# Layer 0's tail: ScalarE normalises the next batch's x, each front has the bank of its own projection tile, and VectorE takes two modulations

## The reference, cut to what matters

```python
def _sln(h, w, ln_g, ln_b, Wg, bg, Wb, bb):          # layer norm, scaled and shifted by a condition
    mu = jnp.mean(h, axis=-1, keepdims=True)
    var = jnp.mean((h - mu) ** 2, axis=-1, keepdims=True)
    ln = (h - mu) / jnp.sqrt(var + EPS) * ln_g + ln_b
    gamma = (w @ Wg.T + bg)[:, None, :]
    beta = (w @ Wb.T + bb)[:, None, :]
    return gamma * ln + beta
h = _sln(hidden, w, ...)
qkv = (h @ Wqkv.T + bqkv)
...                                                  # attention, 16 heads of 32
out = out @ Wp.T + bp
h1 = out + hidden
h2 = _sln(h1, w, ...)
return h2 + h1
```

## Time and profile before

| | |
|---|---|
| median of three executions | 2795.2 us |
| profiled execution, its time | 2797.68 us |
| its span, first to last instruction | 2795.9 us |
| TensorE busy | 2621.9 us (94%) |
| VectorE busy | 2162.2 us (77%) |
| ScalarE busy | 1830.6 us (65%) |
| GpSimd busy | 1964.9 us (70%) |
| mean granted TensorE clock | 0.975 |

### The profile page before, as it was taken

The page is one execution under the profiler, slowest core; times in us unless marked ns, Lnnn a source line. Parts: engine busy times, 40 slices in busy tenths (PEclk is TensorE's granted clock), DMA queues, the critical chain, the costliest instruction groups (busy, mean ns, idle before and its releaser), DMA issues. The chain is left out here.

```text
span 2795.9 us, 59973 instructions
## 1 busy us (share of the span) xinstructions
PE 2621.9 (94%) x21716; PEld 1469.8 (53%) x21761; DVE 2162.2 (77%) x4455; ACT 1830.6 (65%) x3302; POOL 1964.9 (70%) x1579
## 2 busy tenths in 40 slices
PE   7899989999999999999959998999899989987998
PEld 5655566554665547655425554555455445543443
DVE  5777768777687777877667778777877787768997
ACT  4366664665656655566656677667766776667996
POOL 0298844897449873598748986988798778965542
PEclk9999999999999999999979999999999999999999
DMA  6122343224432244323232313321432132245444
GB/s 234 39 58 59 125 135 121 58 62 152 125 103 59 60 146 139 97 62 92 85 81 50 84 41 106 81 59 32 118 81 59 35 108 58 62 156 185 109 102 109
DMA packets 168764, 260.42 MB, mean 93 GB/s; under 512 B 85388, under 2 KB 91668, under 8 KB 167576
## 3 DMA queue, kind: packets, MB, share of 16 engines
q1 hardware_dynamic: 166680, 250.27, 32.7%
q0 software_dynamic: 1792, 6.33, 0.6%
HBM read 99.15 MB, written 38.88 MB: 49 GB/s over the span
## 5 line engine op out<-in xcount | busy, mean ns | idle before, releaser
L547 DVE TENSOR_REDUCE a_mxs<-ps 128x1 f32<-128x512 f32 x2048 | 1268.2, 681 | 258.7 <-PE ps L414 256.3
L508 ACT ACTIVATE a_p<-ps 128x512 f32<-128x512 f32 x2048 | 1043.5, 606 | 205.1 <-PE ps L428 194.8
L368 POOL TENSOR_TENSOR a_sum<-a_p 128x512 f32<-128x512 f32 x736 | 939.0, 1285 | 204.2 <-PE ps L448 114.5
L414 PE MATMUL ps<-a_k,a_q 96*128 96x512 f32 x2048 | 854.8, 424 | 25.3 <-DVE a_mxs L547 21.0
L428 PE MATMUL ps<-a_q,a_k 98*128 98x512 f32 x2048 | 808.7, 419 | 15.7 <-ACT a_p L508 9.8
L448 PE MATMUL ps<-a_sum,a_unit 128*32 128x512 f32 x1536 | 650.5, 596 | 0.6 <-POOL a_sum L368 0.6
L374 POOL TENSOR_TENSOR a_sum<-a_sum,a_p 128x512 f32<-128x512 f32 x480 | 618.4, 1288 | 37.6
L448 PE MATMUL ps<-a_p,xv 128*32 128x512 f32 x3968 | 639.0, 595 | 0.0
L414 PEld LDWEIGHTS ps<-a_k,a_q 96*128 96x128 f32 x2048 | 389.7, 190 | 259.7 <-DVE a_mxs L547 105.5
L428 PEld LDWEIGHTS ps<-a_q,a_k 98*128 98x128 f32 x2048 | 384.2, 189 | 242.3 <-ACT a_p L508 144.7
L517 ACT ACTIVATE a_ots<-ps 128x512 f32<-128x512 f32 x256 | 152.6, 598 | 403.5 <-PE ps L448 402.5
(11 more groups left out here) (250 smaller groups left out, 3103.9 us busy)
## 6 DMA issues: line engine op xcount, KB each, us to landing
a_q<-qh SPq DMA_DIRECT2D x256, 128.0 KB, 2.3
a_k<-kh SPq DMA_DIRECT2D x256, 128.0 KB, 2.4
a_q<-ql SPq DMA_DIRECT2D x128, 128.0 KB, 2.4
a_k<-kl SPq DMA_DIRECT2D x128, 128.0 KB, 2.4
x<-a_p SPq DMA_DIRECT2D x64, 256.0 KB, 2.1
a_p<-in_w_fc SPq DMA_DIRECT2D x12, 1024.0 KB, 8.0
kh<-in_x SPq DMA_DIRECT2D x4, 2048.0 KB, 14.6
a_p<-x SPq DMA_DIRECT2D x16, 512.0 KB, 5.9
```

Of the source, the lines that this page charges most:

```text
L368: pair = pool.tensor_tensor(tile, keys[0], keys[1], ALU.add)
L414: pe.matmul(self.mx[self.mx_ring[at]], self.q[j][0:96, t * P:(t + 1) * P], self.k[j][0:96, half * HALF:(half + 1) * HALF], start=True, sto ...
L508: act.activation(self.key_tile(u, kt), self.st[self.st_ring[CHUNKS * k + n]], ACT.Exp, scale=self.scale).then_inc(self.s_exp, 1)
L547: dve.reduce_max(self.mxs[:, k % 2, c:c + 1], self.mx[self.mx_ring[CHUNKS * k + c]], axis=AX.X).then_inc(self.s_mxr, 1)
```

## The change

ScalarE normalises the next batch's x, two tiles in each of the first four rounds of its tail loop, from a negative mean times reciprocal (`nmx`) that VectorE forms for all 8 tiles in one small instruction. For b > 0 front n takes bank `Y_BANK[n]`, and waits for the gamma product of tile n (n < 6) or the residual sum of tile n (n = 6, 7). Units 0 to 3 take banks 3, 4, 5 and 0, and the later ones 1, 2, 6 and 0 in turn; unit v < 4 waits for `rest` v. Fronts 5 and 7 are modulated once on VectorE in place (`exact`) and copied by ScalarE (`Copy`) instead of being modulated twice on ScalarE. At t = 5 `modulate` now stands ahead of `absolute`. Batch 0's own front is as before.

```diff
+        nmx = sb("nmx", [P, TT], FP32)
...
-        FRONT_BANK = lambda b: (3, 4, 5, 0, 3, 4, 5, 1) if b else tuple(range(UN))
+        FRONT_BANK = lambda b: Y_BANK if b else tuple(range(UN))
+        EXACT = lambda b: (5, 7) if b else (4, 5, 6, 7)
+        exacts = lambda b, n: 4 * min(b, 1) + 2 * max(b - 1, 0) + sum(i < n for i in EXACT(b))
...
-        BANKS = ((0, 1, 2, 6),) + ((6, 2, 0, 1),) * (B - 1)
-        bank = lambda b, v: BANKS[b][v % 4]
+        BANKS = (0, 1, 2, 6)
+        bank = lambda b, v: Y_BANK[v] if b and v < 4 else ((1, 2, 6, 0) if b else BANKS)[v % 4]
...
-                        if b and n < 4:
+                        if b and n < 6:
                             pe.wait_ge(s_gm, TT * (b - 1) + n + 1)
-                        elif b and n < 7:
-                            pe.wait_ge(s_trD, UN * b + n - 4 + 1)
                         elif b:
-                            pe.wait_ge(s_gm, TT * (b - 1) + Y_BANK.index(FRONT_BANK(b)[n]) + 1)
+                            pe.wait_ge(s_h1, TT * (b - 1) + n + 1)
...
-                        if v == 0 and b:
-                            pe.wait_ge(s_h1, TT * (b - 1) + Y_BANK.index(bank(b, 0)) + 1)
-                        elif v == 0:
-                            pe.wait_ge(s_trD, UN * b + 1)
-                        if v == 1 and b:
-                            pe.wait_ge(s_gm, TT * (b - 1) + Y_BANK.index(bank(b, 1)) + 1)
-                            pe.wait_ge(s_h1, TT * b)
+                        if v < 4:
+                            pe.wait_ge(s_trD, UN * b + v + 1)
...
-                        if c and b == 0:
-                            act.wait_ge(s_trG, k + 1)
+                        if n in EXACT(b):
+                            act.wait_ge(s_trG, exacts(b, n) + 1)
                             act.activation(to, at, ACT.Copy).then_inc(s_trA, 1)
                             continue
...
+                    def normalize(t):
+                        act.wait_ge(s_nmx, b + 1)
+                        act.activation(xn[:, t, :], xn[:, t, :], ACT.Identity, bias=nmx[:, t:t + 1], scale=rs[0][:, t:t + 1]).then_inc(s_z, 1)
...
                     for t in range(TT + 5 if last else TT + 1):
+                        if not last and t < TT // 2:
+                            normalize(2 * t)
+                            normalize(2 * t + 1)
...
+                        if not last and 4 <= t:
+                            modulate(b + 1, (t - 4,))
                         if not last and t in (3, 5):
                             act.wait_ge(s_ss, TT * b + t - 2 + 1)
                             absolute(b + 1, (t - 3) // 2)
-                        if not last and 4 <= t:
-                            modulate(b + 1, (t - 4,))
...
                     if not last:
-                        normalize(ch, b + 1)
+                        dve.wait_ge(s_sd, b + 2)
+                        ch.mark(dve.reciprocal(rs[0][:, :], sd[0][:, :]))
+                        ch.wait()
+                        dve.scalar_tensor_tensor(nmx[:, :], mv[0][:, :, 0], -1.0, rs[0][:, :], ALU.mult, ALU.mult).then_inc(s_nmx, 1)
+                        ch.close()
...
                     if not last:
+                        for n in EXACT(b + 1):
+                            exact(b + 1, n)
                         for n in range(4, UN):
                             rest(b + 1, n)
```

More of the change, by code:

```diff
@@ L688, in layer0 @@
         s_dqt, s_dqrow = sem("dq_t_ps"), sem("dq_row_ok")
-        s_gm = sem("gamma")
+        s_gm, s_nmx = sem("gamma"), sem("nmx")
         s_rr, s_xr, s_vl = sem("root_inv"), sem("x_rooted"), sem("v_last")
@@ L1019, in batch @@
                             pe.wait_ge(s_trA, UN * b + KC * (v // 2 + 1))
-                        if v == 0 and b:
-                            pe.wait_ge(s_h1, TT * (b - 1) + Y_BANK.index(bank(b, 0)) + 1)
-                        elif v == 0:
-                            pe.wait_ge(s_trD, UN * b + 1)
-                        if v == 1 and b:
-                            pe.wait_ge(s_gm, TT * (b - 1) + Y_BANK.index(bank(b, 1)) + 1)
-                            pe.wait_ge(s_h1, TT * b)
+                        if v < 4:
+                            pe.wait_ge(s_trD, UN * b + v + 1)
                         if v % 4 == 0 and v <= 2 * UN:
                             ready(g, 0)
-                        o = v - len(BANKS[b])
+                        o = v - len(BANKS)
                         if o >= 2 * UN:
@@ L1258, in normalize, with exact @@
                     ch.close()
-                def exact(b, k):
-                    n = KC + k
+                def exact(b, n):
+                    k, at = HALVES[n][1], ps[:, FRONT_BANK(b)[n], :]
                     dve.wait_ge(s_tr, UN * b + n + 1)
-                    dve.tensor_scalar(ps[:, n, :], ps[:, n, :], mod_col(b, 0, k), mod_col(b, 1, k), ALU.mult, ALU.add).then_inc(s_trG, 1)
+                    dve.tensor_scalar(at, at, mod_col(b, 0, k), mod_col(b, 1, k), ALU.mult, ALU.add).then_inc(s_trG, 1)
                 def rest(b, n):
@@ L1267, in rest @@
                     dve.wait_ge(s_trA, UN * b + n + 1)
-                    if b or c == 0:
-                        dve.wait_ge(s_trF, UN * b - KC + n + 1 if b else k + 1)
+                    if n not in EXACT(b):
+                        dve.wait_ge(s_trF, UN * b + n + 1 - exacts(b, n))
                     dve.tensor_tensor(h_lo[:, 4 * c:4 * c + 4, k, :], ps[:, FRONT_BANK(b)[n], :].rearrange("p (t c) -> p t c", c=P),
@@ L1276, in modulate @@
                         if half == 0:
-                            exact(b, k)
+                            exact(b, KC + k)
                         rest(b, KC * half + k)
```

## The result

The changed kernel takes 2774.2 us (median of four runs, 2772.19 to 2775.84) against 2794.8 for the kernel before on the same chip: a ratio of 0.9924, 95% interval 0.9912 to 0.9936, 20.6 us less. The forecast was 2774.8. The profiled execution took 2772.19 us with a span of 2770.4; it is the fastest of its four.

A forecast was written before the change was run, and what follows sets the result against it. TensorE, 94% busy, was taken as the bound, its idle gaps in the tails delaying the units. Three tails x 6.8 = 20.4 us off the 2795.2 median forecast 2774.8, range 2770 to 2785.

The forecast's parts named there:

- VectorE's block and the first gap: First tail: VectorE's 7.03 us normalising xn goes, front 0 starts at 354.8 instead of 357.97, and 3.2 us gap goes.
- No half clock behind front 0: Projection 4, behind front 0: without a gap TensorE's clock stays full and the eight records save 1.54 us.
- The pace of 3.87 us a tile, no stall at fronts 1 to 3: TensorE's first tail: one tile costs 3.87 us; gamma 1, 2 and 3 are out before their fronts want them.
- a sign of being wrong: TensorE ahead of front 5: a gap of more than 1.2 us would show the prediction wrong.
- Banks: Fronts 5 and 6 in the tail: their waits on `rest`, 4.0 us, go; a new 1.2 us wait replaces them.
- Unit 0 and unit 2: End of first tail: unit 0 starts at 375.2 instead of 382.06; unit 2 7.5 or 6.7 us earlier, 6.8 taken.
- the slow case: Unit 0's first eight matmuls run as behind earlier gaps, 1.7 us more; unit 2 starts at 382.4, 6.7 us earlier.
- The prediction's third mark: Start of unit 2 in the third tail: 1072.1 less three times 6.8 us gives 1051.7.
- The two modulations on VectorE: Tail's end: ScalarE trades 2 x 1.32 for 2 x 0.6 less a wait of 0.9, about 0.5 us gained.
- ScalarE's air: ScalarE between 348.4 and 381.1 in the first tail: 28.5 us of work, so 4.2 us of air.
- The third rival: ScalarE becomes the bound: 2780 at 1.4 us per xn instruction, 2803 if weights also land late; chance of slower 0.06.
- What lies behind: Units after the start of unit 2: banks, stores and sums come in time, so the advance is kept.

## Why the prediction was right

**VectorE's block and the first gap.** Right. Front 0 was expected at 354.8 and came at 354.95 on the clock of before (353.92 + 1.03); 0.27 us of the gap is left. The price of an xn instruction on ScalarE, taken from L1204, was 0.70 start to start and measured 0.71. The run with xn back on VectorE brings back the 3.29 us and the half clock; the run with xn alone moved shows 13.6 us.

**No half clock behind front 0.** Right: 3.60 us.

**The pace of 3.87 us a tile, no stall at fronts 1 to 3.** Right. Front 4 was expected at 370.3 and came at 370.46, and the new wait ahead of front 5 at 1.2 and was 1.26, which is a hair over the 1.2 that the prediction names as a sign of being wrong.

**Banks.** Right. The waits on `rest` are gone, and without the new banks the changed kernel loses 11.5 us; the kernel with nothing but xn moved, which has the old banks too, is 6.8 to 7.1 us behind the changed one.

**Unit 0 and unit 2.** Unit 0 was expected at 375.2 and came at 375.36. Here the one term was mis-sized: I chose the slow case for its first eight matmuls, some 1.7 us more a tail, because TensorE would idle 2.8 of 4.3 us ahead of it. It did idle 2.8, in two pieces of 1.26 and 1.51 with the fronts between, and the clock stayed at its upper level: the first group took 1.20 us instead of 2.06. Unit 2 came at 381.85, between my 381.6 and 382.4, so a tail gave 7.2 to 7.4 us instead of 6.8, 21.8 in the three instead of 20.4. The prediction's third mark, 1051.7, came at 1050.2. The medians differ by 20.6 and, on another chip, by 20.7, some 1.2 us less than the tails of the traces show. No run says where that lies; it is well inside the interval of the ratio (18 to 25 us). So the mechanism was forecast and the sum was near, but that the forecast is met to 0.6 us is partly luck: 1.4 us too little for the clock, and 1.2 us of the traces' gain that the medians don't have.

**The two modulations on VectorE.** Right that copy 5 waits under 1 us for VectorE (0.9 expected, 0.78 measured) and that little is gained; the run without them shows no gain.

**ScalarE's air.** Right: doubling the eight instructions costs 7.2 us; the 2.1 us a tail that I had walked through for them at 1.4 us each is 6.3. The third rival, with the Trainium skill's rule ("ScalarE: Activation LUTs", "Rules for kernel authors") behind it, had the cost of one instruction right, 0.80 us long against 541 ns, and the effect on the kernel wrong.

**What lies behind.** Right: none of the advance was given back in the units. From unit 2 of one tail to the end of projection 3 in the next the traces have 307.2 and 307.0 us before, 306.9 and 307.1 after, and from the third unit 2 to the end 1723.8 before and 1721.3 after.

**Missed.** Gamma 6 at 0.68 us; it took 1.69. It cost nothing here because the fronts no longer waited for what stands behind it, and gamma 7 had to wait for ScalarE's normalisation of tile 7 (out at 375.66) in any case. With the old banks it did cost, 1.0 us a tail. The small instruction that forms `nmx` took 0.72 us, not 0.2, which nothing waited for.

## What to carry to other kernels

Read which engine's queue the late instruction stands in, and what stands ahead of it that nobody needs yet; moving such work to an engine with air gained here although each instruction got dearer there (0.55 to 0.71 us). Run the parts of a change alone before saying that they need each other: 13.6 and 4.9 us here, against 20.6 for both. Where two engines hold each other up, as VectorE and GpSimd do here, an instruction that starts 0.1 us later can take 1 us more, so look at lengths after each reordering, not only at the order.

## What the runs showed of the hardware

A VectorE and a GpSimd instruction that both read two tiles in SBUF don't slow each other evenly. In the rows above the one that started first had its normal length (0.68 or 1.26 us) and the other was held up: 1.79 for GpSimd when VectorE led by 0.02 us, 1.69 for VectorE when GpSimd led by 0.12. VectorE's normalisation of xn, with one input in SBUF, is held up as well: its block of eight takes 7.03 us, the first 4.9 of them beside GpSimd, and single ones up to 1489 ns; with GpSimd kept away the block takes 3.7 us and none of the eight more than 550 ns. The Trainium skill, "SBUF — State Buffer", section "Who interferes with whom", says that of an instruction of VectorE that needs the pair of ports shared with GpSimd and one of GpSimd, whichever issues first holds it to its end and the other is blocked. The traces agree with it.

The sum of TensorE's idle time did not decide alone whether the granted clock fell. Behind single gaps of 3.28 and 3.29 us it dropped to half, 1.2 GHz (5.14 and 5.30 us for eight records; the granted clock of the kernel before is 0.50 from 359 to 361 us); behind 1.63 and 1.68 us it did not (3.60). Gaps of 1.86 and 2.15 us with one front between gave half clock for fronts 6 and 7 and the first group of unit 0, and in some tails for the second group too. Gaps of 1.26 and 1.51 us with three fronts between gave none, and neither did 1.85 and 1.56 with three fronts between, though these add up to 3.41, more than the single gap of 3.28.
